# Value products of two key tiles placed together, and one attention's tail summed by TensorE, in a twelve-layer Perceiver kernel

## What is computed

```python
# block 0: each latent token picks 16 context rows
idx = clip(floor(sigmoid(query @ W_pts + b_pts) * n), 0, n - 1)
w = softmax(query @ W_w + b_w)
deform = input[idx] * w[..., None]
kh, vh = deform @ W_k + b_k, deform @ W_v + b_v      # 16 heads of 16
att = softmax(einsum('bchd,bcphd->bchp', qh, kh) / sqrt(e))
out = einsum('bchp,bcphd->bchd', att, vh).reshape(bs, C, e) @ W_o + b_o

# block 1 (block 3: unit-length q and k, a learned scale, an added bias and no mask)
scores = einsum('bhqd,bhkd->bhqk', Q, K) / scale
attention = softmax(where(mask, scores, NEG_INF))
out = einsum('bhqk,bhkd->bhqd', attention, V) @ W_proj.T + b_proj
```

## Time and profile before

| | us |
|---|---|
| median of 3 runs | 2580.96 |
| lowest and highest | 2580.65 and 2588.36 |
| the profiled execution, its own time | 2592.84 |
| its span, first to last instruction | 2591.1 |
| TensorE busy | 2336.5 (90%) |
| VectorE busy | 1659.7 (64%) |
| ScalarE busy | 1247.6 (48%) |
| GpSimd busy | 812.4 (31%) |

### The profile page before, as it was taken

One profiled execution on the slowest core, in us unless ns is written; L12 is line 12 of the kernel. 1 busy time (PEld: TensorE's weight loads), 2 busy tenths in 40 slices (PEclk: granted clock), 3 DMA queues, 4 the chain that ended last, 5 costly groups with the idle time before them and its releaser, 6 DMA issues. The chain is left out here.

```text
span 2591.1 us, 44514 instructions
## 1 busy us (share of the span) xinstructions
PE 2336.5 (90%) x17351; PEld 1491.9 (58%) x17398; DVE 1659.7 (64%) x3204; ACT 1247.6 (48%) x2071; POOL 812.4 (31%) x661
## 2 busy tenths in 40 slices
PE   8866779999998889999999999699789999998898
PEld 6734446666663455666655666356456666666554
DVE  6976365455538855888888854644666565554577
ACT  3325135444544325555555553676345555554465
POOL 5610052233204302322233300055444444342154
PEclk9978899999998989999999999899899999999999
DMA  4201353323205046767776663133322222120132
GB/s 117 66 1 33 108 160 92 85 70 100 65 14 165 1 106 129 140 119 145 148 140 129 115 113 68 54 98 98 105 62 68 71 78 84 45 64 22 63 92 64
DMA packets 358594, 226.44 MB, mean 87 GB/s; under 512 B 289913, under 2 KB 326610, under 8 KB 358386
## 3 DMA queue, kind: packets, MB, share of 16 engines
q1 hardware_dynamic: 355314, 215.20, 34.5%
q0 software_dynamic: 3072, 8.39, 1.1%
HBM read 114.87 MB, written 0.52 MB: 45 GB/s over the span
## 5 line engine op out<-in xcount | busy, mean ns | idle before, releaser
L100 PE MATMUL PS<-hot 128*128 128x512 f16 x460 | 139.6, 442 | 82.9 <-DVE l0a_g L1087 17.5
L3917 POOL TENSOR_TENSOR l2x_rows<-l2x_rows,l2x_one 128x256 f16<-128x256 f32 (+1 forms) x91 | 89.1, 1005 | 382.4 <-DVE l2x_rows L1475 355.5
L4021 PE MATMUL PS<-l2x_rows,l2x_pth 128*128 128x512 f16 x832 | 200.4, 379 | 2.6 <-DVE l2x_mean L4230 2.6
L3675 DVE CUSTOM_DVE_ANT_0 l1x_junk<-PS,l1x_bias 128x1024 bf16<-128x1024 f32 (+1 forms) x128 | 123.2, 992 | 96.1 <-PE PS L3336 95.2
L4223 DVE TENSOR_TENSOR l2x_pl<-l2x_sc,l2x_ph 128x1664 f16<-128x1664 f32 x64 | 124.3, 1942 | 45.9 <-ACT l2x_ph L4100 45.3
L3675 DVE CUSTOM_DVE_ANT_0 l3x_junk<-PS,l3x_bias 128x1024 bf16<-128x1024 f32 (+1 forms) x128 | 123.7, 991 | 45.9 <-PE PS L3336 44.8
L4208 DVE CUSTOM_DVE_ANT_0 l2x_sc<-PS,l2x_bias 128x1665 f32<-128x1665 f32 x64 | 120.9, 1889 | 38.6 <-issue 37.5
L4118 ACT ACTIVATE l2x_meanT<-PS 128x256 f32<-128x256 f32 x64 | 24.5, 383 | 250.2 <-PE PS L3983 250.2
L3546 ACT ACTIVATE l3x_pT<-PS 128x512 f32<-128x512 f32 x144 | 84.5, 594 | 120.3 <-PE PS L3382 117.9
L100 PEld LDWEIGHTS PS<-hot 128*128 128x128 f16 x460 | 46.2, 110 | 155.8 <-issue 44.4
L3975 PE MATMUL PS<-l2x_kh,l2x_qth 128*128 128x512 f16 (+1 forms) x512 | 131.9, 339 | 1.5 <-issue 1.5
(11 more groups left out here) (858 smaller groups left out, 6230.7 us busy)
## 6 DMA issues: line engine op xcount, KB each, us to landing
l2f_unit<-in_L_ffn_units_dram SPq DMA_DIRECT2D x36, 384.0 KB, 3.0
l3f_unit<-in_L_ffn_units_dram SPq DMA_DIRECT2D x34, 384.0 KB, 3.0
l1x_kst<-l1x_kh SPq DMA_DIRECT2D x128, 100.1 KB, 2.2
l3x_kst<-l3x_kh SPq DMA_DIRECT2D x128, 100.1 KB, 2.2
l2x_rows<-in_ctx_dram SPq DMA_DIRECT2D x8, 1536.0 KB
l1x_ctx<-in_ctx_t_dram SPq DMA_DIRECT2D x7, 1601.0 KB, 7.4
l3x_ctx<-in_ctx_t_dram SPq DMA_DIRECT2D x7, 1601.0 KB, 6.7
l1x_kst<-l1x_kl SPq DMA_DIRECT2D x64, 100.1 KB, 2.2
```

The lines of the kernel that those rows point to most:

```text
L100: self.nc.tensor.matmul(self.PS[:, bank, :], self.hot[:, 0:P], self.hot[:], start=True, stop=True)
L3675: v.tensor_tensor_reduce(junk[:, slot(it), 0:n], slot_banks(it)[:, 0:n], bias[:, 0 if normed else b % 2, at:at + n], 1.0, LOWEST, ALU.add, ...
L3917: last = nc.gpsimd.tensor_tensor(high[:, at], of[:, at], one[0:p, at].unsqueeze(2).unsqueeze(3).to_broadcast([p, i, NC, P]), ALU.mult)
L4021: nc.tensor.matmul(PS[:, ACC, :], pth[:, u % 2, m, :], rows2[:, b % 2, :, :, m, :], start=(m == 0), stop=False)
```

## The change

In the large cross attentions `pT` gets three buffers, and the values of two tiles stand together behind each even tile: behind tile 2 those of 0 and 1, behind tile 4 those of 2 and 3, and so on to 10 and 11 behind tile 12; those of tile 12 stay where they were, behind tile 0 of the next batch. The buffer `raw` is dropped, and `xnT`, which is free by then, takes its place. In the first cross attention, for tile 3 TensorE sums the weighed values itself: products of each point with the identity, added in PSUM, which also turn them, in three parts behind a new semaphore `part_weighed`; for tile 2 it does so with the eight points that are left after the even and the odd addition. GpSimd's last addition goes.

```diff
-                turn_out(NT - 2)
-                project(NT - 2)
-                turn_out(NT - 1)
-                project(NT - 1)
+                def sum_out(t, points, first, last):
+                    of = ([bv[:]] if first else []) + [val[:, t % SLOTS, p, :] for p in points]
+                    for j in range(NC):
+                        for i, a in enumerate(of):
+                            mm = nc.tensor.matmul(PS[:, SUM_BANK[t] + j, 0:P], a[:, j * P:(j + 1) * P], k.ident[:],
+                                                  start=(first and i == 0), stop=(last and i == len(of) - 1))
+                    return mm
+                t = NT - 2
+                pe.wait_ge(r_low, NT * PAIRS)
+                pe.wait_ge(even_summed, 1)
+                sum_out(t, range(0, 4), True, False)
+                pe.wait_ge(odd_summed, t + 1)
+                sum_out(t, range(4, 8), False, True).then_inc(o_turned, 1)
+                project(t)
+                t = NT - 1
+                pe.wait_ge(k_used, NT * PAIRS)
+                for i in range(3):
+                    pe.wait_ge(part_weighed, i + 1)
+                    last = sum_out(t, range(4 * i, 4 * i + 4), i == 0, i == 2)
+                last.then_inc(o_turned, 1)
+                project(t)
...
+                t = NT - 1
+                shares(t)
+                for part in (0, 1):
+                    weigh(t, part).then_inc(part_weighed, 1)
+                weigh(t, 2)
+                link(weigh(t, 3))
+                of = val[:, t % SLOTS, :, :]
+                v.tensor_tensor(of[:, 8:12, :], of[:, 8:12, :], of[:, 12:16, :], ALU.add).then_inc(part_weighed, 1)
+                add(NT - 2)
                 add(NT - 1)
...
+    PT = 3
...
-        pT = sb("pT", [P, 2, G2, BANK])
-        raw = sb("raw", [P, BANK])
+        pT = sb("pT", [P, PT, G2, BANK])
+        raw = xnT[:, 0, :]
...
-                        for g in range(G2):
-                            if m > 0:
-                                values(b, m - 1, g)
-                            elif b > 0:
-                                values(b - 1, KT - 1, g)
+                        if m == 0:
+                            ready = [(b - 1, KT - 1)] if b > 0 else []
+                        else:
+                            ready = [(b, m - 2), (b, m - 1)] if m % 2 == 0 else []
+                        for b_, m_ in ready:
+                            for g in range(G2):
+                                values(b_, m_, g)
...
-                        if e >= 2 * G2:
-                            act.wait_ge(summed, e - 2 * G2 + 1)
+                        if e >= PT * G2:
+                            act.wait_ge(summed, e - PT * G2 + 1)
```

More of the change, by code:

```diff
@@ L338, in layer_0_xattn @@
         Y_BANK, O_BANK, K_BANK, V_BANK = 2, 3, 4, 6
+        SUM_BANK = {NT - 2: 0, NT - 1: K_BANK}
         SPARE = 3
@@ L487, in keep_o @@
                     act.wait_ge(o_turned, t + 1)
-                    nc.scalar.activation(oT[:, t, :, :].rearrange("p c n -> p (c n)"), PS[:, O_BANK, 0:D], ACT.Copy).then_inc(o_copied, 1)
+                    if t in SUM_BANK:
+                        nc.scalar.activation(oT[:, t, :, :], PS[:, SUM_BANK[t]:SUM_BANK[t] + NC, 0:P], ACT.Copy).then_inc(o_copied, 1)
+                    else:
+                        nc.scalar.activation(oT[:, t, :, :].rearrange("p c n -> p (c n)"), PS[:, O_BANK, 0:D], ACT.Copy).then_inc(o_copied, 1)
                 def weigh(t):
@@ L602, in even @@
                     of = val[:, t % SLOTS, :, :]
-                    link(v.tensor_tensor(of[:, 0:4, :], of[:, 0:4, :], of[:, 8:12, :], ALU.add))
+                    return v.tensor_tensor(of[:, 0:4, :], of[:, 0:4, :], of[:, 8:12, :], ALU.add)
                 def all_four(t):
@@ L632, in tail @@
                         link(weigh(t, 0))
+                    elif m == 5 and t == NT - 2:
+                        even(t).then_inc(even_summed, 1)
+                    elif t == NT - 2:
+                        pass
                     elif m == 5:
-                        even(t)
+                        link(even(t))
                     elif m == 6:
@@ L3097, in context_attention @@
             qsq = junk[:].rearrange("p a n -> p (a n)").bitcast(F32)
-            q_high = raw[:].bitcast(F16).rearrange("p (t r f) -> p t r f", t=NT, r=R)
+            q_high = raw.bitcast(F16).rearrange("p (t r f) -> p t r f", t=NT, r=R)
             qn2 = sb("qn2", [P, NT * H])
@@ L3536, in exp @@
                     e = (b * KT + m) * G2 + g
-                    to = pT[0:n, (b * KT + m) % 2, g, :]
+                    to = pT[0:n, (b * KT + m) % PT, g, :]
                     if m in ON_VECTOR:
@@ L3703, in add_bias @@
                     dve.wait_ge(turned_made, e + 1)
-                    if e >= 2 * G2:
-                        dve.wait_ge(summed, e - 2 * G2 + 1)
-                    to = pT[0:n, (b * KT + m) % 2, g, :].rearrange("p (u s) -> p u s", s=S)
+                    if e >= PT * G2:
+                        dve.wait_ge(summed, e - PT * G2 + 1)
+                    to = pT[0:n, (b * KT + m) % PT, g, :].rearrange("p (u s) -> p u s", s=S)
                     of = PS[0:n, S_BANK + g, :].rearrange("p (u s) -> p u s", s=S)
```

4 lines of the change are left out of this document (2 added, 2 removed).

## The result

The changed kernel takes 2597.05 us, median of 5 runs (2593.78 to 2598.43), beside 2583.52 us for the kernel before (5 runs, 2580.65 to 2588.36). The ratio is 1.0051, 95% interval 1.0040 to 1.0063: slower by 0.5%, some 13 us. In the experiments a difference in us is worked out from the ratio, and the difference of the two medians can be an us or two off it. The profiled execution took 2597.64 us, span 2595.8.

What follows compares the result with a forecast made beforehand. TensorE was taken to bound both large cross attentions, a VectorE chain the first one's tail. Block 1 +6.3, block 3 +10.1 and tail -8.1 make +8.3 on the median 2580.96: 2589.3 us, range 2568 to 2600.

Steps and rivals of the forecast that it cites:

- Bound and edges: Large cross attentions: TensorE bounds; each removed separate block of values saves 0.22 us, 96 in all, 21 us.
- Block 1's walk: Block 1, pairs of tiles followed through the timeline: seven batches +4.1 us, the last +2.2, together +6.3.
- the +1.3: Block 1, even batches with O and P items, which take a slot and are read late: +1.3 us each.
- Block 3's walk: Block 3, pairs of tiles followed through the timeline: seven batches of 1.13 us plus 2.2, together +10.1.
- The example of V in tile 2: Block 3, tiles 1 and 2: V waits for its slot, wins 0.21 us, and the pair ends 0.66 later.
- The tail: End of the first cross attention: last addition at 155.95 instead of 164.02, at full TensorE clock; -8.1 us.
- The up to 0.5 us for the next layer: Layer behind the tail: its first products may find the full clock and win up to 0.5 us.
- Buffers: Large cross attentions: the third buffer costs nothing; in none of the pairs is a buffer the last wait.
- The first (edges won, nothing laid bare): Rival, whole change: separate blocks saved without new waits; -29 us, 2552; 8%.
- The second (half of the walked waits covered): Rival, both layers: other work covers half the new waits; 18.5 us less than forecast, 2571; 12%.
- The third: Rival, tail of the first cross attention: TensorE's clock stays at half; +6 us on the forecast, 2595; 8%.
- The fourth: Rival, 84 pairs with items: VectorE's queue falls behind, 0.15 us or more each; +12.6 us, 2602; 8%.

Runs made afterwards that it cites:

- large_only: The changed kernel with the tail of the first cross attention as before; 2604.48 us, ratio 1.0082 against the kernel before.
- chosen_pairs: The changed kernel, but pairing only tiles (1,2), (3,4) in block 1 and (2,3), (5,6) in block 3, none in last batches; 2582.43 us, ratio 0.9993.
- large_again: The same kernel as large_only, one execution on another chip, for its profile; 2599.4 us.
- the two short kernels: The kernel before, and large_only, each with VectorE's row maximum over a quarter of the columns; 2568.21 and 2568.13 us.

## Why the prediction was right, and where it was off

Forecast +8.3, measured +13.5 (by the ratio's interval 10 to 16): the sign and the mechanism hold, 2597 is inside the range, and the sum was some 5 us too low. The median lies 7.8 above the 2589.3 of the forecast; 2.6 of that is the kernel before, whose median is 2583.52 over five runs and was 2580.96 over three.

- **Bound and edges.** An edge pair is worth 0.22, a second block in a row 0.87: confirmed. Where nothing is laid bare a pair gains 0.23, in the first seven batches of block 1 at tiles (4,5). Each layer's trace has 55 separate blocks of values instead of 103, 96 fewer in all as counted; the forecast's 112 for 208 left out that the last blocks of a layer run together.
- **Block 1's walk.** Forecast 4.1 for the seven batches and 2.2 for the last. The seven measure 0.07 + 3 x 0.31 + 3 x 1.00 = 4.0. In this the odd batches cost 0.31 instead of 0.05, and the even ones 1.00 instead of 1.3: in them (4,5) gains 0.23 as in the odd ones, and the loss of 0.54 stands at (2,3), where an A item waits 0.46 for ScalarE. The prediction gives the +1.3 without its parts, so which of them was too high isn't on record. That the two errors nearly cancel is luck. The last batch, in after, is 0.87 + 0.66 + 3 x 0.23 - 0.64 = 1.6 in the stream, the last term because the values of tile 10 now follow the last scores; with their 0.87 in the closing part it is 2.4. Sum 6.4, forecast 6.3.
- **Block 3's walk.** Forecast 7.9 and 2.2. The first seven batches lose 1.07 to 1.44 each, 8.4 in all, and the last 1.8 in the stream and 0.87 in the closing part: 11.1 instead of 10.1. The example of V in tile 2 gave 0.66 and measured 0.66 or 0.67; too low were (6,7) in the odd batches (+0.45 for +0.2) and the last batch.
- **The term left out: the clock in the large layers.** The prediction took it as full throughout, as the windows of before show, and priced the new waits by their length alone. In after one stretch at half clock costs 1.6 in the stream of block 3; in large_only three cost 4.6. The closing part of block 3 takes 8.93 instead of 7.33 at a mean clock of 0.84 instead of 1.00; 0.87 of this is the values of tile 10, and the other 0.7 is the clock. This 0.7 may be chance: chosen_pairs, without pairs there, has 8.28 instead of 7.33, and large_again, with them, none of it.
- **The tail.** Working and end were right (first weighing 145.95 for 146.1; weighings of 1.16 us on the mean for 1.2; the third part waits for VectorE; full clock), the length 14.6 for 14.4. Timed alone it gives -6 and -8.5 around the forecast of -8.1. The up to 0.5 us for the next layer can't be seen: that layer takes 80.5 to 84.3 with the new tail and 81.8 to 83.6 with the old one.
- **Buffers** at nothing: confirmed.
- **Rivals.** The first (edges won, nothing laid bare) falls with large_only. The second (half of the walked waits covered): the losses add up to what was walked, or a little more. The third: the tail had the full clock. The fourth, VectorE falling behind by 0.15 a pair: didn't happen, in the odd batches of block 1 every pair agrees with the walk within 0.08, in block 3 within 0.25.
- **The account.** Walk +6.4 and +11.1, a stretch at half clock +1.6, the clock in the closing part +0.7 at most, tail -6 to -8.5: +10.6 to +13.8, beside 10 to 16 measured. The streams and the closing parts are those of one execution, and the parts between differ by chance by several us.

## What to carry to other kernels

An item that shows no wait may still be standing right behind one: before work is moved away from in front of it, compare its start with the end of what it needs, since the cover is worth only that distance. A gain is to be read from one point where both kernels stand alike to the next, not to a cut that a wait may step over, and one found beside a loss holds only beside it; what held exactly was a gain with nothing else changed ahead of it. And a wait of a microsecond may cost more than its length, when the clock falls behind it.

## What the hardware showed that I had not expected

- The granted clock fell to the lower level behind gaps of 0.6 and 1.1 us in one batch and stayed full behind the same gaps in another of the same execution: 1.03 us against 1.87 for M, 1.94 against 2.71 for a double block. What decides it stays open.
- As long as the clock is full, the order of waits repeats to 0.01 us between executions and chips, all through block 1 (382.60 or 382.61 in four profiles). In block 3 single batches differ by 0.1 to 0.3, in the two short kernels by up to 0.9; where the profile names a releaser, it is the transfer of an A item's keys. The runs of one kernel differ by far more than this, by 4 to 14 us.
- Four weighings took 4.63 us with GpSimd idle, where three took 5.76 beside its addition.
